# Attended values of a latent-attention kernel: high and low latents side by side in the stationary tile, two heads in 512 moving columns

## What is computed

```
x = x + attn(layernorm(x));  x = x + moe(layernorm(x))
q = x@Wq (16 heads of 128+64, the 64 rotated)      kv = x@Wkv_a -> 64 latents (layernorm, gamma, beta), 64 rotated key values
k, v = latents@Wkv_b (128 + 128 for each head)      attn = softmax(q k^T / sqrt(192)) v @ Wout
moe: 8 experts of width 176, the best two of a softmax gate, and a shared expert of width 352
```

## Time and profile before

| | us |
|---|---|
| median of 3 runs | 818.66 (813.7 to 818.84) |
| span of the profiled execution, first to last instruction | 811.2 |
| its own whole time | not given apart from the span |
| start of x2 in sequence 4, and in sequence 5 | 386.28 and 480.62 |

### The profile page before, as it was taken

How to read it: one execution, slowest core, us unless ns; L and a number is a source line. 1 busy time by engine, 2 the same in 40 slices (tenths; PEclk the granted TensorE clock), 3 DMA queues, 4 the chain that set the end, 5 groups by cost and what they waited for, 6 DMA issues and landing times.

```text
span 811.2 us, 17956 instructions
## 1 busy us (share of the span) xinstructions
PE 764.0 (94%) x5924; PEld 716.2 (88%) x5924; DVE 544.3 (67%) x1269; ACT 437.8 (54%) x1158; POOL 507.8 (63%) x587
## 2 busy tenths in 40 slices
PE   8969899999999999999999999999999999999997
PEld 6769888999899988999899998999889998999986
DVE  6679886597538964398736975389644987369442
ACT  3678753685319851396316853197513964169421
POOL 5448467683658746585656836587465856569154
PEclk9999999999999999999999999999999999999999
DMA  8930000000000000000000000000000000000000
GB/s 237 293 106 2 1 14 1 29 1 15 2 1 26 0 13 0 13 13 0 13 0 26 0 13 0 0 26 0 13 0 14 12 0 13 0 14 1 1 2 13
DMA packets 20226, 18.76 MB, mean 23 GB/s; under 512 B 2816, under 2 KB 19680, under 8 KB 20192
## 3 DMA queue, kind: packets, MB, share of 16 engines
q1 hardware_dynamic: 19360, 18.13, 7.4%
q10 hardware_dynamic: 832, 0.21, 0.1%
HBM read 16.23 MB, written 2.10 MB: 23 GB/s over the span
## 4 chain that ended last, share of the span: by engine, by line
PE 40%; POOL 24%; issue 19%; DVE 7%; ACT 3%; POOLq 1%; DVEq 0%; ACTq 0%
PE ps_q L245 18%; PE ps_y L245 11%; POOL probs L1394 11%; POOL qswap L1384 6%; POOL qf L1389 5%; PE ps_t L1001 3%; PE ps_s L245 3%; PE ps_o L245 2%; DVE q_lo L305 1%; PE ps_t L926 1%; ACT qswap L1084 1%; DVE qf L1212 1%; DVE nmax L1221 1%; PE ps_o L887 1%; DVE pT_lo L305 1%
## 5 line engine op out<-in xcount | busy, mean ns | idle before, releaser
L1394 POOL TENSOR_TENSOR probs<-probs,rinv 128x512 f32<-128x512 f32 x128 | 131.6, 1041 | 56.3 <-DVE rinv L1225 56.3
L400 POOL TENSOR_TENSOR pT_hi<-probs,one 128x256 fp32r<-128x256 f32 x112 | 75.4, 673 | 112.4 <-DVE probs L1320 92.4
L1166 ACT ACTIVATE probs<-ps_q 128x256 f32<-128x256 f32 (+1 forms) x112 | 42.8, 383 | 184.4 <-PE ps_q L245 183.7
L1110 ACT ACTIVATE probs<-ps_s,nmax 128x256 f32<-128x256 f32 x256 | 119.4, 478 | 14.7 <-DVE nmax L1221 13.6
L1317 DVE TENSOR_TENSOR probs<-ps_q,probs 128x256 f32<-128x256 f32 x88 | 37.3, 424 | 128.9 <-ACT probs L1166 128.8
L1389 POOL TENSOR_TENSOR qf<-qf,qswap 128x512 f32<-128x512 f32 x63 | 91.8, 1458 | 17.5 <-DVE qf L1212 9.2
L1084 ACT ACTIVATE qswap<-ps_q 32x512 f32<-32x512 f32 x128 | 75.6, 591 | 46.7 <-PE ps_q L245 45.0
L305 DVE TENSOR_TENSOR pT_lo<-ps_t,pT_hi 128x512 fp32r<-128x512 f32 x128 | 86.9, 679 | 13.5 <-ACT pT_hi L1084 13.3
L1384 POOL TENSOR_TENSOR qswap<-qswap,qsin 128x512 f32<-128x512 f32 x63 | 81.1, 1287 | 21.3 <-ACT qswap L1084 21.3
L1221 DVE TENSOR_REDUCE nmax<-ps_s 128x2 f32<-128x512 f32 x128 | 87.5, 684 | 10.3 <-PE ps_s L245 8.3
L245 PE MATMUL ps_s<-kT_hi,q_hi 128*128 128x256 f32 x256 | 78.8, 308 | 12.5 <-DVE q_lo L305 8.8
(11 more groups left out here) (208 smaller groups left out, 2524.0 us busy)
## 6 DMA issues: line engine op xcount, KB each, us to landing
wq_raw<-Wq_dram SPq DMA_DIRECT2D x16, 192.0 KB, 4.2
xnext<-x_dram SPq DMA_DIRECT2D x8, 256.0 KB, 2.8
wout_raw<-Wout_dram SPq DMA_DIRECT2D x8, 256.0 KB, 4.9
xin<-x_dram SPq DMA_DIRECT2D x8, 256.0 KB, 2.7
out_dram<-x SPq DMA_DIRECT2D x8, 256.0 KB, 2.2
mg_raw<-w_gate_dram SPq DMA_DIRECT2D x4, 352.0 KB, 6.7
mu_raw<-w_up_dram SPq DMA_DIRECT2D x4, 352.0 KB, 7.0
md_raw<-w_down_dram SPq DMA_DIRECT2D x3, 384.0 KB, 6.7
```

What stands on the lines that cost most here:

```text
L400: return gp.tensor_tensor(hi, src, ones.to_broadcast(list(src.shape)), ALU.mult)
L1110: last = nc.scalar.activation(probs[h % 3][:, j, :], L.ps_s[h % 2][:, j, :], ACT.Exp, bias=nmax[:, h, j:j + 1], accum_out=rsum[:, h, j:j + 1])
L1166: nc.scalar.activation(gate[m % 2][0:rows, :], L.ps_q[m % 2][0:rows, 0, :], ACT.Silu).then_inc(ev.silu_done.sem, 1)
L1394: gp.tensor_tensor(probs[h % 3][:, :, :], probs[h % 3][:, :, :], rinv[:, h, :].unsqueeze(2).to_broadcast([P, NT, S]), ALU.mult).then_inc(e ...
```

## The change

The latents' high and low part stand side by side in one tile `kv`, and one matmul takes both heads of a pair as 512 moving columns. Rows 0 to 63 of ps_o then hold the product with the high latents, rows 64 to 127 that with the low latents, for two heads beside each other (128 x 512, the whole bank). ScalarE copies the two quarters that stand in the wrong rows into `ocross`, VectorE adds them to the other two, ScalarE rounds the sum and GpSimd makes its low part.

```diff
-        self.kv_hi, self.kv_lo = (sb(f"kv_{x}", [P, NT, 3, RANK], F32R) for x in ("hi", "lo"))
+        self.kv = sb("kv", [P, NT, 2, RANK], F32R)
...
-                zeros = L.kp[:, :, :].rearrange("p j (n c) -> p j n c", c=RANK)
-                nc.vector.tensor_copy(L.kv_hi[:, :, 0:3:2, :], zeros)
-                nc.vector.tensor_copy(L.kv_lo[:, :, 0:3:2, :], zeros).then_inc(L.events.zeros_set, 1)
...
-        pT_hi, pT_lo = ([sb(f"pT_{x}{n}", [P, NT, S], F32R) for n in range(3)] for x in ("hi", "lo"))
-        o_hi, o_lo = ([sb(f"o_{x}{n}", [P, S], F32R) for n in range(2)] for x in ("hi", "lo"))
+        pT_hi, pT_lo = ([sb(f"pT_{x}{n}", [P, NT, 2, S], F32R) for n in range(2)] for x in ("hi", "lo"))
+        ocross = L.krot[:, :, :, :].rearrange("p n j f -> p (n j f)")
+        osum = [xhat_f[:, n, :] for n in range(2)]
+        o_hi, o_lo = ([t[:, n, :] for n in range(2)] for t in (xf_hi, xf_lo))
...
-        cT = o_hi[0][0:CK, :]
+        cT = sb("cT", [CK, S], F32R)[:, :]
...
-            def attend(i, h):
...
+            def attend(i, p):
+                pe.wait_ge(ev.plo_done.sem, ev.plo_done.upto(i, 2 * p + 2))
+                pe.wait_ge(ev.osum_done.sem, ev.osum_done.upto(i, p))
...
+                terms = [(part[p % 2], c) for part in (pT_hi, pT_lo) for c in range(NT)]
+                for n, (part, c) in enumerate(terms):
+                    last = nc.tensor.matmul(L.ps_o[:, :, :], L.kv[:, c, :, :].rearrange("p n c -> p (n c)"), part[:, c, :, :],
+                                            start=n == 0, stop=n == len(terms) - 1)
...
-                    if due(r - 1):
-                        attend(i, 2 * (r - 1))
                     if due(r):
                         turn(i, 2 * r)
                     if due(r - 1):
-                        attend(i, 2 * (r - 1) + 1)
+                        attend(i, r - 1)
...
+            def attended_cross(i, p):
+                act.wait_ge(ev.pv_done.sem, ev.pv_done.upto(i, p + 1))
+                if p >= 1:
+                    act.wait_ge(ev.osum_done.sem, ev.osum_done.upto(i, p))
+                copy(ocross[upper, :], L.ps_o[low, 0, :])
+                copy(ocross[low, :], L.ps_o[upper, 1, :]).then_inc(ev.ocross_done.sem, 1)
...
             def attended_hi(i, p):
-                act.wait_ge(ev.pv_done.sem, ev.pv_done.upto(i, 2 * p + 2))
+                act.wait_ge(ev.osum_done.sem, ev.osum_done.upto(i, p + 1))
...
-                copy(o_hi[p % 2][:, :], L.ps_o[:, 0, :]).then_inc(ev.ohi_done.sem, 1)
+                copy(o_hi[p % 2], osum[p % 2]).then_inc(ev.ohi_done.sem, 1)
...
+                    if due(r - 2):
+                        attended_hi(i, r - 2)
                     if prep and r == NP:
                         prep_x(i + 1)
                     if due(r - 1):
-                        attended_hi(i, r - 1)
+                        attended_cross(i, r - 1)
...
-            def attended_lo(i, p):
-                dve.wait_ge(ev.ohi_done.sem, ev.ohi_done.upto(i, p + 1))
-                minus_hi(o_lo[p % 2][:, :], L.ps_o[:, 0, :], o_hi[p % 2][:, :]).then_inc(ev.olo_done.sem, 1)
+            def attended_sum(i, p):
+                dve.wait_ge(ev.ocross_done.sem, ev.ocross_done.upto(i, p + 1))
...
+                for n, rows in enumerate((upper, low)):
+                    last = vec.tensor_tensor(osum[p % 2][rows, :], L.ps_o[rows, n, :], ocross[rows, :], ALU.add)
+                last.then_inc(ev.osum_done.sem, 1)
...
+            def attended_lo(i, p):
+                pool.wait_ge(ev.ohi_done.sem, ev.ohi_done.upto(i, p + 1))
+                gp.tensor_tensor(o_lo[p % 2], osum[p % 2], o_hi[p % 2].bitcast(F32),
+                                 ALU.subtract).then_inc(ev.olo_done.sem, 1)
...
-                for r in range(NP - 1):
-                    normal(i, 2 * (r + 1))
+                for r in range(NP + 2):
+                    if due(r + 1):
+                        normal(i, 2 * (r + 1))
                     if prep and r == NP // 2:
                         power(L.var_a, L.rstd_a, ev.vara_done, ev.rsa_done, i + 1)
-                    normal(i, 2 * (r + 1) + 1)
+                    if due(r - 2):
+                        attended_lo(i, r - 2)
+                    if due(r + 1):
+                        normal(i, 2 * (r + 1) + 1)
```

More of the change, by code:

```diff
@@ L93, in __init__ @@
         self.t_full = count("t_full", NH)
-        self.pv_done = count("pv_done", NH, head=NH)
+        self.pv_done = count("pv_done", NP, head=NP)
         self.gu_full = count("gu_full", CH)
@@ L124, in __init__ @@
         self.qlo_done = count("qlo_done", NP)
-        self.olo_done = count("olo_done", NP, head=1)
+        self.olo_done = count("olo_done", NP)
+        self.ocross_done = count("ocross_done", NP)
+        self.osum_done = count("osum_done", NP, head=1)
         self.max_done = count("max_done", NH)
@@ L545, in _ @@
                 ev = L.events
-                for events in (ev.su_done, ev.cb_done, ev.ulo_done, ev.qcos_done, ev.exp_done, ev.pv_done, ev.olo_done, ev.osb_done,
+                for events in (ev.su_done, ev.cb_done, ev.ulo_done, ev.qcos_done, ev.exp_done, ev.pv_done, ev.osum_done, ev.osb_done,
                                ev.out_stored):
@@ L834, in loop @@
         comb2 = sb("comb2", [P, NT, P])
-        cT = o_hi[0][0:CK, :]
+        cT = sb("cT", [CK, S], F32R)[:, :]
         gate, prod, unit = ([probs[n][:, m, :] for m in range(NT)] for n in range(3))
-        u_hi, u_lo = ([t[:, 0, :] for t in ring] for ring in (pT_hi, pT_lo))
-        half = (slice(1, 3), slice(0, 2))
+        u_hi, u_lo = ([ring[0][:, 0, 0, :], ring[0][:, 0, 1, :], ring[1][:, 0, 0, :]] for ring in (pT_hi, pT_lo))
+        upper, low = slice(0, RANK), slice(RANK, P)
         even, odd = slice(RANK, RANK + HR), slice(RANK + HR, P)
@@ L927, in turn @@
                 last.then_inc(ev.t_full.sem, 1)
-            def attend(i, h):
-                p, n = divmod(h, 2)
-                pe.wait_ge(ev.plo_done.sem, ev.plo_done.upto(i, h + 1))
-                if n == 0:
-                    pe.wait_ge(ev.olo_done.sem, ev.olo_done.upto(i, p))
-                if h == 0:
+            def attend(i, p):
+                pe.wait_ge(ev.plo_done.sem, ev.plo_done.upto(i, 2 * p + 2))
+                pe.wait_ge(ev.osum_done.sem, ev.osum_done.upto(i, p))
+                if p == 0:
                     pe.wait_ge(ev.kvlo_done.sem, ev.kvlo_done.upto(i, 1))
-                both = "p n c -> p (n c)"
-                last = three(L.ps_o[:, 0, :],
-                             [(kv_hi[:, c, half[n], :].rearrange(both), kv_lo[:, c, half[n], :].rearrange(both),
-                               pT_hi[h % 3][:, c, :], pT_lo[h % 3][:, c, :]) for c in range(NT)], start=n == 0, stop=n == 1, skip=True)
+                terms = [(part[p % 2], c) for part in (pT_hi, pT_lo) for c in range(NT)]
+                for n, (part, c) in enumerate(terms):
+                    last = nc.tensor.matmul(L.ps_o[:, :, :], L.kv[:, c, :, :].rearrange("p n c -> p (n c)"), part[:, c, :, :],
+                                            start=n == 0, stop=n == len(terms) - 1)
                 last.then_inc(ev.pv_done.sem, 1)
```

29 lines of the change are left out of this document (16 added, 13 removed).

## The result

The changed kernel takes 899.25 us (median of 4 runs, 888.26 to 910.74) against 818.75 us for the kernel before beside it (4 runs too): a ratio of 1.0886, 95% interval 1.0799 to 1.0973. The forecast was 847.5 us (811 to 862). Slower is right, the size is not: +29 us was forecast, and +80 came out by the medians, +72 by the ratio.

What follows compares the result with a forecast made beforehand. Four engines at 91 to 95% were taken to bound the attention, VectorE's rounds setting the first stretch. 1.7 + 1.8 + 0.1 gave 3.6 us per sequence, 28.8 for eight, hence 847.5 us (811 to 862).

Steps and rivals of the forecast that it cites:

- load less relief, rounds: Up to turn(15): VectorE's added sums cost 1.7 us, GpSimd's later turn(15) 0.1; TensorE's saving becomes waiting.
- Rival A: Whole kernel: TensorE is the bound after all, its saving counts in rounds 1 to 8; 802 us, chance 0.15.
- rival B: First stretch: engines have slack for the load, its gain of some 1.8 us cancels the tail; 818 us, chance 0.13.
- so I count the subtraction's duration and no stall: GpSimd's queue: the new subtraction finds its o_hi ready, so it costs only its 0.73 us per pair.
- The stated sign: Rounds: TensorE would wait on normals, pT_lo or q_lo for 3 us or more per sequence.
- GpSimd gives the same: First stretch: followed through GpSimd's queue, the added subtractions make turn(11) about 2 us late, matching VectorE's sum.
- +1.7 remains: First stretch: six VectorE sums at 0.33 cost 2.0 us per sequence, less 0.3 taken up by idle time.
- I count +0: turn(15) to the end of attend(7): TensorE's 0.48 us saving is set against pair 6's sum (0.66) ahead of pT_lo(15).
- the tail: End of attend(7) to project(7): crossings, sums, o_hi and GpSimd's low part take about 2.7 us, +1.8 per sequence.
- Rival C: Behind project(7): the clock falls while TensorE stands still, 1 to 2 us per sequence; 856 to 863 us, chance 0.12.
- the matmul's price: attend on TensorE: a 512-column matmul costs 0.24 us, so four take 0.96 per pair, 0.48 saved.
- a longer q_lo: VectorE's q_lo: more GpSimd work may lengthen it, up to 1.5 us per sequence, 12 in all; 0 taken.

Runs made afterwards that it cites:

- e12: Changed kernel with GpSimd's low part moved ahead of its normal and project one round later on TensorE: 879.63 us, one run.
- e4: Kernel before plus, per pair, two ScalarE copies, one VectorE addition and one GpSimd subtraction, results unused: 855.8 us, ratio 1.0513.
- e5: Kernel before with attend cut from 12 to 8 matmuls per pair, low latents' product left out: 825.77 us beside 824.95 for before.
- e1: Changed kernel with GpSimd's attended_lo moved ahead of the normal in its round: 863.28 us, ratio to before 1.0616.
- e7: Changed kernel with GpSimd's low part ahead of its normal, plus 18 unused matmuls on TensorE ahead of the last project: 883.1 us.
- e8: Kernel before plus two ScalarE copies of 64 x 256 per pair, results unused: 842.73 us, ratio 1.0349.
- e9: Kernel before plus one VectorE addition of 64 x 256 per pair, result unused: 832.72 us (821.94, 843.49).
- e10: Kernel before plus one GpSimd subtraction of 128 x 256 per pair, for which nobody waits: 834.27 us (826.17, 842.37).
- e2: Changed kernel with project one round later on TensorE, GpSimd left alone: 875.09 us, ratio 1.0605.

## Why the prediction was right in its direction and wrong in its size

| term, us in sequence 4 | forecast | measured | by |
|---|---|---|---|
| load less relief, rounds | +1.8 | +2.7 | e12; e4 and e5: 3.34 - 0.83 = 2.5 |
| order in the queues, rounds | 0 | +2.7 | after less e12; e1 alone 2.4 |
| turn(15) to the end of attend(7) | 0 | +0.68 | timelines |
| chain at the end | +1.8 | +2.07 | timelines |
| clock in project(7) | 0 | +0.69 | timelines, e7 |
| expert stage | 0 | +0.26 | marks |
| sum | 3.6 | 9.1 | spacing: +9.06 |

- **Right: what bounds the kernel.** Four full engines in a ring, TensorE's 94% no bound by itself. Rival A (TensorE the bound, 802 us) falls by e5, which gives 1.1 us for 3.8 saved, and rival B (cancelled) by e4, where the loads that it took for hidden cost 5.2 us. e8, e9 and e10 each load one engine of three and each makes the rounds longer.
- **Wrong, the largest: "so I count the subtraction's duration and no stall".** I asked who stands behind the subtraction in GpSimd's queue and whether its input is there. Both were answered rightly: its input is there. I didn't ask who waits for its own result, and from where in that queue. The section on the kernel even had the place: `project` "two rounds later". As it stands ahead of turn(2q + 6) on TensorE and its low part behind normal(2q + 6) on GpSimd, the delay follows from the two lists. The stated sign, waits of TensorE on normals, pT_lo and q_lo of 3 us or more, didn't come (2.0 us in the rounds of sequence 4); 6.4 us of waits on the low part came in their place. e1 and e12 show what the order costs: 2.4 to 2.7 us, some 21 us of the whole time. Not all of it is `project`'s wait, as e2 and e12 side by side show: the delay that the subtraction gives to what stands behind it had been counted, but as one and the same lateness with VectorE's ("GpSimd gives the same").
- **Wrong: the first stretch by VectorE alone, "+1.7 remains", "GpSimd gives the same".** ScalarE's +0.54 for a pair was worked out and then stood in no sum. It was the dearest of the three, 2.15 us by e8, and too small as well: two copies in a row start 0.39 us apart and not 0.27, so that the change adds 0.95 us for a pair. VectorE's one addition costs 1.0 (e9) where 1.7 was taken, GpSimd's 1.0 (e10). The combined load is 3.3 where 1.8 had been summed; the relief, counted at nothing, gives 0.8 back. VectorE's two sums are 0.55 us for a pair in the change, and e4 and e9 have but 0.33 of it, so 3.3 is rather low.
- **Wrong: "I count +0" from turn(15) to attend(7).** The mechanism had been named (the sum ahead of pT_lo(15)), and then was set off against TensorE's 0.48. It costs 0.68 net.
- **Right, slightly small: the tail.** Each hop is there in its order. The two crossings took 0.77 us in place of 0.64 and the two sums 0.86 in place of 0.74, which is the difference: neither pair overlaps as assumed. From the end of attend(7) to project(7) it is 3.0 us, 2.7 had been forecast.
- **Rival C** was right in place, beside the forecast: TensorE stands 2.3 us and the clock then is 0.51 for 3.4 us. In the whole loop of after the granted clock falls 12 times, for 44 us; before, 3 times, for 10 us. C was too dear, 1 to 2 us a sequence where 0.7 and at most 0.26 appear, and e7's filler gained hardly any of it.
- **Right: the matmul's price,** 0.23 us for 0.24.
- **Did not occur: a longer q_lo.** The 12 us kept for it were none:

```profile
L307 DVE TENSOR_TENSOR q_lo<-qf,q_hi x64: 674/882/1765, 56.2 to 821.1; 128x512 fp32r<-128x512 f32 x64
```

The median is 882 ns against 1218, with more work on GpSimd. It may be that GpSimd's instructions fall elsewhere in the rounds and fewer stand beside q_lo; that wasn't measured. The rule on the shared ports in the Trainium skill ("SBUF — State Buffer", Who interferes with whom) is not refuted by this, but it can't be priced by the sum of GpSimd's work.

The range (811 to 862) was too narrow, because its upper end held only costs that I had listed, and no allowance for a wait that I had not listed.

Open: how the price of the order divides between `project`'s wait and GpSimd's other work in the changed kernel itself; why the clock falls more often in it; what the kernel would do if the two halves in ps_o could be added without the copies of ScalarE, which was not tried.

## What to carry to other kernels

When an instruction is moved to another in-order engine, check the order against both sides: not only whether its inputs are there and who stands behind it, but where its reader stands in its own queue against the readers of what is ahead of it. Here one swap of two calls was worth 2.4 us of 103. And when several engines are all over 90% busy, work taken from one is worth little (here 1.1 of 3.8 us) while work given to the others is paid in part everywhere (in rounds and end together 3.4 of ScalarE's 6.2 us, 1.4 of VectorE's 2.6, 1.0 of GpSimd's 5.8), so each added piece needs a term of its own in the sum, and a load counted as hidden must be named with what hides it.

## What was not expected of the hardware

The setup ahead of the loop can run at half the clock. Windows of the same 8 us in e9 and in e8, which differ only in the loop:

```profile
16.00:24.00 8.00, 8.00 (x31) 6.12 (x30) 3.69 (x9) 2.94 (x8) 6.86 (x15) 0.50 0.88 246
```

```profile
16.00:24.00 8.00, 7.95 (x56) 6.59 (x56) 6.28 (x18) 5.34 (x14) 7.05 (x15) 1.00 1.00 283
```

31 matmuls in place of 56 at a clock of 0.50, with TensorE busy throughout; turn(0) of the first sequence then comes at 80.3 us in place of 57.6. In e9 the clock is at 0.50 all the way from 12.0 to 66.6 us, with TensorE busy for 52.1 of these 54.6 us. Nothing in these runs says why; the marks of one sequence inside the loop are not touched by it.
